# Row scatters wait on two alternating semaphores, at most two in flight: a convolution and mixture-of-experts kernel

## The reference

```python
x = x + conv_ref(_ln_c(x), ...)           # x: (64, 64, 16, 16) f32
t = _to_tokens(x)                          # 16384 tokens of 64 channels
flat = _ln_t(t)
probs = softmax(flat @ router_w.T)         # 8 experts
topk_probs, topk_idx = top_k(probs, 2)
gates = topk_probs / (sum(topk_probs) + 1e-9)
h = silu(flat @ w1[e].T) * (flat @ w3[e].T)   # hidden size 682
y = h @ w2[e].T
t = t + sum over the two chosen e of gate * y
```

## Time and profile before

| | us |
|---|---|
| median of 3 runs | 916.5 |
| lowest, highest | 914.6, 918.02 |
| span of the profiled execution | 1186.4 |

### The profile page before, as it was taken

One profiled execution on the slowest core, in us unless ns is written; L12 is line 12 of the kernel. 1 busy time (PEld: TensorE's weight loads), 2 busy tenths in 40 slices (PEclk: granted clock), 3 DMA queues, 4 the chain that ended last, 5 costly groups with the idle time before them and its releaser, 6 DMA issues.

```text
span 1186.4 us, 17267 instructions
## 1 busy us (share of the span) xinstructions
PE 878.8 (74%) x4403; PEld 559.4 (47%) x4403; DVE 592.8 (50%) x1392; ACT 528.3 (45%) x999; POOL 562.5 (47%) x574
## 2 busy tenths in 40 slices
PE   7687714417648887885878888878689999999924
PEld 4533503214525454452544444544345666778723
DVE  6955703306864444443444444444345566555546
ACT  6544301103335444543444444444345666555546
POOL 3400467571004665665566656655465444444453
PEclk9788856658859898988988978988799999999965
DMA  8700302112323333332333323323233434666547
GB/s 188 127 0 1 113 22 74 31 64 66 117 83 124 104 124 96 119 102 83 96 94 113 105 89 117 105 89 115 63 119 117 134 124 141 222 204 216 184 176 249
DMA packets 75219, 133.78 MB, mean 113 GB/s; under 512 B 15989, under 2 KB 48942, under 8 KB 75152
## 3 DMA queue, kind: packets, MB, share of 16 engines
q1 hardware_dynamic: 55952, 111.83, 29.9%
q0 software_dynamic: 19200, 21.28, 6.6%
HBM read 99.67 MB, written 29.71 MB: 109 GB/s over the span
## 4 chain that ended last, share of the span: by engine, by line
PE 60%; issue 15%; DVE 9%; another core or an unknown queue 7%; ACT 6%; DMA 1%; POOL 0%; DVEq 0%; ACTq 0%; SPq 0%; POOLq 0%
PE bank L1369 29%; PE bank L1383 15%; PE bank L1271 4%; DVE conv_all L1136 3%; ACT y_and_rows L739 3%; PE bank L1348 3%; PE bank L1395 2%; PE bank L1285 2%; PE bank L1290 1%; ACT conv_all L706 1%; PE bank L1211 1%; PE bank L1325 1%; PE bank L1216 1%; ACT quant_tmp L646 1%
## 5 line engine op out<-in xcount | busy, mean ns | idle before, releaser
L1369 PE MATMUL bank<-xT_hi_lo,w 128*128 128x512 f32 (+1 forms) x748 | 302.3, 404 | 99.2 <-DVE conv_all L1136 80.6
L706 ACT ACTIVATE conv_all<-bank 128x512 f32<-128x512 f32 (+1 forms) x408 | 235.9, 597 | 268.4 <-PE bank L1369 181.2
L1136 DVE TENSOR_TENSOR conv_all<-conv_all,bank 128x512 f32<-128x512 f32 x340 | 224.0, 684 | 260.7 <-ACT conv_all L706 96.6
L548 POOL DMA_INDIRECT expert_rows<-y_and_rows,slot_all x256 | 249.2, 973 | 174.3 <-DVE slot_all L1018 97.6
L1369 PE MATMUL bank<-xT_lo_hi,w 128*128 128x512 f32 (+1 forms) x748 | 284.7, 381 | 0.0
L558 POOL DMA_INDIRECT result_rows<-conv_all,dest_all x144 | 144.7, 1005 | 244.3 <-DVE conv_all L1143 204.5
L1369 PEld LDWEIGHTS bank<-xT_hi_lo,w 128*128 128x128 f32 x748 | 143.1, 191 | 196.4 <-DVE conv_all L1136 100.3
L1383 PE MATMUL bank<-conv_all,w 128*64 128x512 f32 (+1 forms) x680 | 214.9, 673 | 15.6 <-issue 11.8
L558 POOL DMA_INDIRECT result_rows<-squares,dest_all x128 | 128.7, 1006 | 144.5 <-DVE squares L1143 104.3
L1369 PEld LDWEIGHTS bank<-xT_lo_hi,w 128*128 128x128 f32 x748 | 143.8, 192 | 20.6
L1383 PEld LDWEIGHTS bank<-conv_all,w 128*64 128x64 f32 x680 | 59.4, 159 | 122.6 <-issue 119.0
(11 more groups left out here) (257 smaller groups left out, 1110.3 us busy)
## 6 DMA issues: line engine op xcount, KB each, us to landing
w<-expert_w SPq DMA_DIRECT2D x68, 704.0 KB
w<-expert_w SPq DMA_DIRECT2D x68, 192.0 KB
conv_all<-expert_rows SPq DMA_DIRECT2D x56, 132.0 KB
expert_w<-w_stacked SPq DMA_DIRECT2D x8, 704.0 KB
w_split<-expert_w SPq DMA_DIRECT2D x6, 704.0 KB
w_stacked<-expert_w SPq DMA_DIRECT2D x6, 704.0 KB
x_all<-in_x SPq DMA_DIRECT2D x16, 256.0 KB, 4.0
x_all<-y_and_rows POOLq DMA_DIRECT2D x16, 256.0 KB, 4.2
```

What stands on the lines that cost most here:

```text
L548: nc.gpsimd.indirect_dma_start(xs, bass.IndirectOffsetOnAxis(ap=slot_all[:, s, k * GH + g:k * GH + g + 1], axis=0), rows_all[:, s, g, :], ...
L706: nc.scalar.activation(sbuf[k % 3][0:m, :], h1_ps[k % 3][0:m, :], ACT.Silu).then_inc(silu_rdy, 1)
L1136: V.tensor_tensor(hbuf[k][0:m, :], sbuf[k % 3][0:m, :], h3, ALU.mult).then_inc(mul_rdy, 1)
L1369: ins = mm(ps[k % 3][:, rows_], wbuf[i][u][:, 128 * c:128 * c + 128], xT[p][u][:, rows_], start=p == 0, stop=p == 1)
```

## The change

A row scatter adds to the semaphore of its own number's parity, and from the third on it waits until the scatter two before it has landed. The stripe waits go. SP's `scattered` asks both semaphores for half of the scatters.

```diff
             def scattered(stripes):
                 for u in range(2):
-                    sp.wait_ge(scat[u], 16 * 2 * GH * ((stripes + 1 - u) // 2))
+                    sp.wait_ge(scat[u], 16 * GH * stripes)
...
             def scatter_row(i):
                 s, k, g = i // (2 * GH), i % (2 * GH) // GH, i % GH
-                u = s % 2
                 if i % (2 * GH) == 0:
                     wait_apart(pool, slot_rdy, s + 1)
-                    if s >= 2:
-                        wait_apart(pool, scat[u], (s - u) * 128)
+                if i >= 2:
+                    wait_apart(pool, scat[i % 2], 16 * (i // 2))
                 nc.gpsimd.indirect_dma_start(
                     xs, bass.IndirectOffsetOnAxis(ap=slot_all[:, s, k * GH + g:k * GH + g + 1], axis=0),
-                    rows_all[:, s, g, :], None).then_inc(scat[u], 16)
+                    rows_all[:, s, g, :], None).then_inc(scat[i % 2], 16)
```

## The result

| | before | after |
|---|---|---|
| median of 4 runs each, same comparison, us | 916.06 | 985.96 |
| lowest, highest | 914.6, 918.02 | 983.72, 988.15 |
| span of the profiled execution, us | 1186.4 | 981.9 |

The changed kernel is slower: 1.0763 times the time of before, 95% interval 1.0743 to 1.0784, or 70 us. The forecast was 956.5 us, 40 us slower, with 914 to 994 as its range. The direction and the mechanism came as forecast; the size did not, and much of what follows is about the missing 30 us.

A forecast was written before the change was run, and what follows sets the result against it. TensorE was taken to set the pace at 8.88 us a tile, with POOL nearly as full. POOL's lag of 43 + 33 + 28 = 104 us, less 64 hidden by the ring, added 40 to 916.5: 956.5 us, range 914 to 994.

The forecast's parts named there:

- Step 1, the wake-up: On POOL, waking after a blocking wait takes 0.92 us, where the gap between back-to-back scatters is 0.30 us.
- rival of the hidden wait: POOL wakes within the usual 0.30 us gap, 2.4 us fit under 2.56, nothing is late: 916.5 us; chance 15%.
- Step 1, the landing: A row scatter's landing, as seen by a waiting engine, takes between 1.8 and 3.6 us; 2.3 us was taken.
- L: Time from a scatter's start until a waiting engine sees it landed; taken as 2.3 us, every second scatter late by L - 1.64.
- the prediction's formula: Delay of the whole kernel = 92 x (L - 1.64) - 21 us, nothing below L = 1.87.
- Step 2: The burst of 100 row scatters takes 33 us longer; first result scatter at about 292 us, tile 0's load loses next to nothing.
- Step 3: In the 42 tiles with row scatters, each tile's third row scatter is late by 0.66 us, 28 us in all.
- Step 4: POOL's lag at tile 42 becomes 43 + 33 + 28 = 104 us; the result ring hides 64, so DVE and TensorE wait 40.
- second gate: Tile 52's load needs all 256 row scatters and comes 42 us late, which doesn't add to the ring's delay.
- sum of 910 us: The recorded 1186.4 us less stalls of 104 us in routing and 172 us in tiles, against a median of 916.5.
- Far slower: Scatters meet weight transfers more often in timed runs; L = 3.0 on average gives 1020 us; chance 9%.
- result scatters escape the limit: The wait doesn't count result scatters, so up to four of them plus two row scatters are in flight; no term changes.

The follow-up runs named there:

- e4: The changed kernel with one row scatter in flight, each waiting for the one just before, instead of two; 1364.48 us, ratio 1.4895 against the kernel before.
- e9: The kernel before, unedited, recorded once more; 913.29 us, recorded span 911.5 us.
- e5: The changed kernel with eight semaphores, each row scatter waiting for the one eight before, 248 waits; 915.99 us, ratio 1.0005 against the kernel before.
- e10: The changed kernel with 64 row scatters ahead of the first results instead of 100, and 4.7 a tile instead of 3.8; 1018.39 us, ratio 1.1099 against before.

## Why the prediction was right, and where its size was off

**Step 1, the wake-up.** Right as far as a trace can tell. The gaps come as forecast, 0.30 and 0.75 us in turn, and landing and wake-up together take 3.00 us in e4, which is 0.92 us and a landing of 2.1. No row shows the two apart. The rival of the hidden wait falls with the sum: 3.00 us don't fit under 2.56.

**Step 1, the landing, for the burst.** This is the term that was mis-sized. I took L = 2.3 us from bounds of 1.8 and 3.6, because most scatters would find the hardware queue idle. In the quiet stretches they land in 2.1. But on average from 130.83 to 321.66, 99 steps of 1.93 us, L is 2 x 1.93 - 0.92 = 2.94 as the prediction's formula counts it. The stages' DMA shares explain the choice and its error: I leaned on the 0.17 of the stretched recording and added only 0.2 us for the real density of the copies, a share of 0.36 in the first 40 us of after's burst. The 3.6 us of the earlier trace rows was the warning that one landing can be more than half as long again, and nothing weighed how many would be.

**Step 2.** Forecast +33 us and a first result scatter at 292; it came at 322.93, 63.4 us later than in e9, which is 50 x (2.94 - 1.64) = 65. The claim that tile 0's load would lose next to nothing also fell, for the same reason: SyncE issues it at 247.88 where e9 has 233.56, 14 us later. And a longer burst meets more copies: most of its last third now runs beside the first tiles, with a slow landing in each. The first 64 scatters step by 1.81 us (130.83 to 244.55, 63 steps), the other 36 by 2.14 us.

**Step 3.** Right: forecast 0.66 us a tile, 28 us in all. Measured 10.66 - 9.95 = 0.71 us, 29.6 us in all, which is L = 2.35 for this part. The third scatter of a tile does the waiting, as forecast. But few have a landing of 2.35: most wait 0.45 us beyond the usual gap (0.75 - 0.30), and a few slow ones and gaps before the fourth scatter or the results make up the rest. That one average fits is partly luck. The rate of before was forecast at 9.9 us a tile, and is 9.95.

**Step 4.** Right in kind, and its slack of 21 us measured 22.4 in after and 22 to 24 elsewhere. Tile 42's results lag their reduction by 38.5 us in e9 (43 in the prediction), and 93.0 are added: 131.5, less 70.6 of delay, so the ring hid 60.9 us where 64 were forecast. Term by term the sum becomes 38.5 + 63.4 + 29.6 - 60.9 = 70.6 us instead of 43 + 33 + 28 - 64 = 40. The burst alone accounts for 30.4 us of the 30.6; the other three terms are off by -4.5, +1.6 and +3.1, which cancel. (The 60.9 is worked out from the 70.6, so that the sum closes is no check of it; the table above is.)

DVE's reductions do the waiting, as forecast, and TensorE with them; in the tiles with row scatters POOL waits for DVE once at most (1.3 us). Beyond tile 0 the second gate cost nothing to speak of in after: SyncE waits 3.3 us at most for the rows of a later tile.

**The clock of the runs.** The sum of 910 us was right (e9: 911.5), and on it rest all start times above: loop, first results, rate. The reason given for the stall, the rate of the scatters, wasn't: e9 and e5 were recorded at the same rate without it. It belongs to one recording, and the other eleven have spans near their runs' times. That recording as such makes it isn't shown either.

**The rivals.** Far slower (L = 3.0 on average, 1020 us) had the right landing for the burst and the wrong one for the tiles: the burst's L was 2.94 and the tiles' 2.35, so the time lies between it and the forecast. The term that failed is the L of the burst: one value was taken for both stages. That result scatters escape the limit is as described and changed nothing.

The Trainium skill (DMA: Bandwidth & Descriptors, "Anatomy of one DMA — SWDGE (gpsimd) path") gives an estimate of 2.1 us for a scatter of this size. The quiet landings agree (e4, 3.00 - 0.92). The traces show besides what the estimate leaves out, landings of 3.6 us and of some 4.6 us in after's burst. By 2.1 us alone the prediction's formula gives 92 x 0.46 - 21 = 21 us, so by that formula the slower ones make some 49 of the 70.

## What to carry to other kernels

When a kernel limits its asynchronous transfers in flight to N, compare N issue steps with the landing plus the wake-up of the waiting engine, and take the landing beside the kernel's heaviest copies, not the quiet one: here 3 x 1.28 us hid nearly all, 2 x 1.28 missed by half a microsecond in the quiet and by three beside a weight load, and 8 x 1.28 cost nothing. Price such a wait separately for each stage, by the DMA traffic there, and find first what slack the queue behind it has; this one had 23 us, and everything past it went to the end. Before making a slow burst shorter, see what stands behind it in its queue: e10 moved row scatters behind results, and POOL idled 24 us. When a trace's span is far from the runs' time, record the kernel again before working from it.

## What the runs showed of the hardware

An indirect scatter of 34 KB issued by GpSimd landed in 2.1 us when little else moved (e4, 3.00 - 0.92), and in some 4.6 us (after, 5.52 - 0.92) while a 704 KB load was moving. With a single one in flight POOL still waited up to 6.2 us for one (e4).

GpSimd started its next indirect DMA 0.92 us behind the VectorE instruction that released it; behind the landing of a DMA only the sum with that landing is seen, 3.00 us in e4. It started 0.30 us behind its last instruction if the wait was already met (e5). The 248 waits of e5 cost nothing that its runs could find (ratio 1.0005).

The same program was recorded once at 1186.4 us and once at 911.5, while its runs took 916. In the long recording TensorE stood idle 1.8 to 2.5 us before tiny matmuls with nothing recorded that it waited for the earlier trace rows.
